# Halved additions on GpSimd, and the next tile's x turned between context and out-projection

## The reference

```
xn  = layernorm(x)
# attention branch, on xn
q, k, v = split(rmsnorm(xn) * norm1_w @ qkv_w + qkv_b)      # 16 heads of 16
q, k    = relu(q), relu(k), each times cos and sin of the position
ctx     = causal linear attention:  q . cumsum(k v) / (q . cumsum(k) + eps)
h       = xn + ctx @ out_w + out_b
m       = h + gelu((rmsnorm(h) * norm2_w) @ mlp_w1 + mlp_b1) @ mlp_w2 + mlp_b2
# ternary branch, on xn
f       = relu(xn @ Wfc.T + gate * low_rank(xn)) ** 2 @ Wproj.T
out     = x + m + f
```

## Time and profile before

| what | value |
|---|---|
| time, median of 3 runs | 640.94 us (640.76 to 641.73) |
| the profiled execution: time, span | 644.8 us, 641.9 us |
| TensorE busy | 589.1 us (92% of the span), granted clock 0.988 |
| VectorE / ScalarE / GpSimd busy | 421.8 / 367.5 / 217.9 us (66, 57, 34%) |
| HBM traffic | 26 GB/s over the span |

### The profile page before, as it was taken

One profiled execution on the slowest core, in us unless ns is written; L12 is line 12 of the kernel. 1 busy time (PEld: TensorE's weight loads), 2 busy tenths in 40 slices (PEclk: granted clock), 3 DMA queues, 4 the chain that ended last, 5 costly groups with the idle time before them and its releaser, 6 DMA issues.

```text
span 641.9 us, 14501 instructions
## 1 busy us (share of the span) xinstructions
PE 589.1 (92%) x5070; PEld 515.2 (80%) x5070; DVE 421.8 (66%) x776; ACT 367.5 (57%) x654; POOL 217.9 (34%) x219
## 2 busy tenths in 40 slices
PE   2757999989999999999999999999999999999986
PEld 2646878978888888888889887888879888888876
DVE  7689966477655766477664876558674786647542
ACT  5465583546745566465845657455754658455643
POOL 6006333153233432153432432334420533333220
PEclk9969999989999999999999999999999999999999
DMA  7771005600065002620056000740036200540000
GB/s 205 213 188 49 17 1 128 137 2 19 1 150 113 16 0 66 121 74 16 0 122 113 26 16 14 148 100 16 0 90 106 65 16 0 135 94 2 2 1 33
DMA packets 27992, 42.01 MB, mean 65 GB/s; under 512 B 9008, under 2 KB 19904, under 8 KB 27968
## 3 DMA queue, kind: packets, MB, share of 16 engines
q1 hardware_dynamic: 26528, 39.59, 26.7%
q10 hardware_dynamic: 1440, 2.10, 1.2%
HBM read 12.31 MB, written 4.19 MB: 26 GB/s over the span
## 4 chain that ended last, share of the span: by engine, by line
PE 78%; DVE 8%; ACT 6%; issue 2%; SPq 2%; ACTq 1%; DMA 1%; POOL 0%; DVEq 0%
PE accum L1194 20%; PE dense L1179 8%; PE dense L1356 8%; PE shared L1217 5%; DVE wide_lo L945 5%; PE ctx_ps L1242 5%; PE dense L1229 4%; PE dense L1090 4%; PE dense L1361 4%; PE shared L1330 4%; PE shared L1104 3%; PE ctx_ps L1253 2%; PE dense L1094 2%; PE dense L1184 2%; PE upd_ps L1267 2%
## 5 line engine op out<-in xcount | busy, mean ns | idle before, releaser
L945 DVE TENSOR_TENSOR wide_lo<-wide,wide_hi 128x512 fp32r<-128x512 f32 x128 | 116.7, 913 | 81.3 <-ACT wide_hi L672 74.4
L484 POOL TENSOR_TENSOR arena<-arena,tab 128x256 f32<-128x256 f32 x64 | 50.1, 804 | 142.3 <-DMA q_stack<-arena 142.3
L953 DVE TENSOR_TENSOR weighted<-shared,cst 128x512 f32<-128x512 f32 x128 | 82.8, 683 | 18.1 <-PE shared L1217 17.9
L669 ACT ACTIVATE wide<-dense,b 128x512 f32<-128x512 f32 x64 | 44.1, 690 | 80.6 <-PE dense L1361 80.2
L510 POOL TENSOR_TENSOR state<-state,added 128x544 f32<-128x544 f32 x32 | 43.6, 1363 | 115.5 <-DVE added L975 115.5
L1194 PE MATMUL accum<-w_hi,wide_hi 128*128 128x256 f32 x256 | 73.5, 287 | 8.0 <-DVE wide_lo L945 8.0
L1194 PE MATMUL accum<-prT,wide_hi 128*128 128x256 f32 x256 | 66.7, 287 | 6.8 <-DVE wide_lo L945 6.8
L1194 PE MATMUL accum<-w_lo,wide_hi 128*128 128x256 f32 x256 | 71.9, 281 | 0.0
L1194 PE MATMUL accum<-w_hi,wide_lo 128*128 128x256 f32 x256 | 71.8, 280 | 0.0
L659 ACT ACTIVATE wide<-dense,scales 128x512 f32<-128x512 f32 x64 | 44.1, 689 | 43.4 <-PE dense L1184 35.4
L1194 PE MATMUL accum<-prT,wide_lo 128*128 128x256 f32 x256 | 65.2, 281 | 0.0
(11 more groups left out here) (166 smaller groups left out, 1438.5 us busy)
## 6 DMA issues: line engine op xcount, KB each, us to landing
k_stack<-weighted SPq DMA_DIRECT2D x96, 128.0 KB, 2.7
q_stack<-arena SPq DMA_DIRECT2D x184, 64.0 KB, 2.3
xin<-L_attn_x SPq DMA_DIRECT2D x16, 256.0 KB, 2.9
out<-late SPq DMA_DIRECT2D x16, 256.0 KB, 2.3
tab<-trig SPq DMA_DIRECT2D x8, 258.0 KB, 2.7
arena<-L_ffn_w_fc SPq DMA_DIRECT2D x1, 1024.0 KB, 8.5
late<-L_ffn_w_proj SPq DMA_DIRECT2D x1, 1024.0 KB, 7.0
late<-L_attn_mlp_w ACTq DMA_DIRECT2D x1, 1024.0 KB, 5.5
```

The source lines that it names most:

```text
L484: pool.tensor_tensor(q_trig[:, j % 2, r, :, :], qT[:, :, k * P:(k + 1) * P], row.broadcast_to([P, KE, P]), ALU.mult).then_inc(q_trig_done, 1)
L669: act.activation(wide[:, m % 2, :], dense[m % 2][:, :], ACT.Gelu_apprx_tanh, bias=b1[:, m:m + 1]).then_inc(dense_free, 1)
L945: dve.tensor_tensor(wide_lo[:, n % 2, :], wide[:, n % 2, :], wide_hi[:, n % 2, :].bitcast(F32), ALU.subtract).then_inc(lo_done, 1)
L953: dve.tensor_tensor(weighted[:, g, :].rearrange("p (a n) -> p a n", a=4), shared[g % 2][:, :].rearrange("p (a n) -> p a n", a=4), mask.rea ...
```

## The change

What it does, part by part. (1) The four additions of 128 x 1024 on GpSimd are made in halves of 128 x 512, and each half waits until VectorE has done a named `split`: `xn + ob` is made in chunks 1 and 2 instead of ahead of chunk 0; the other six halves stand behind the splits of the MLP blocks 1 to 6. The ternary result goes into `res` and no longer waits for `xb + ctxn`. (2) Turning x of the next tile moves from behind `mlp_up(0)` to between `ffn_up(7)` and the out-projection, and writes the context and update banks (`ctx_ps`, `upd_ps`) instead of `shared`. (3) The four k and q blocks of the next tile move from around `mlp_down(0)`: the first ahead of the turning of h, the second behind it, the two of q behind `ffn_down(7)`; `make_z` moves to behind `mlp_up(1)`. `ffn_down(4)` is no longer halved, and `ffn_up(6)` and `ffn_up(7)` move ahead of and behind the turning of the context. (4) The statistics of the next x move to the very start of the tile on VectorE, the moments behind chunk 0 and the inverse root to chunk 1, `scale_x` on ScalarE into chunk 3 (tile 0: one chunk later, statistics and moments together). (5) SyncE loads x two tiles ahead of its use, behind the 36 stacking DMAs of a tile instead of at its start. Squares and hs are written into `xn` instead of `xs`.

The diff, cut to its core:

```
@@ constants
-        N_SHARED = 26
+        N_SHARED = 24
-        MLP_BEFORE_KQ = 2
...
+        def x_bank(t, m):
+            return shared[m] if isinstance(t, int) and t == 0 else (ctx_ps, upd_ps)[m]
@@ SyncE
+            load_next_x(0)
-            def body(t, more):
+            def body(t, more, more_x):
                 if more:
-                    sp.wait_ge(xn_done, (t + 1) * NB)
-                    sp.wait_ge(xb_done, t + 1)
-                    sp.wait_ge(xs_done, (t + 1) * NB)
-                    load_x(t + 1)
                     sp.wait_ge(q_trig_done, (t + 1) * 2 * NB)
                     sp.wait_ge(v_trig_done, (t + 1) * 2 * NB)
                     load_tab(t + 1)
                     stack(t + 1)
+                if more_x:
+                    load_next_x(t + 1)
@@ GpSimd
-                pool.tensor_tensor(xn[:, :, :], xn[:, :, :],
...
+                def xn_plus_ob(j):
+                    pool.wait_ge(xn_done, (t + 1) * NB)
+                    pool.wait_ge(lo_done, t * 2 * HB + j + 2)
+                    two = slice(2 * j - 2, 2 * j)
...
+                    if 1 <= j <= 2:
+                        xn_plus_ob(j)
+                    if more and j == (2 if isinstance(t, int) and t == 0 else 1):
+                        inverse_root(t + 1)
...
-                if more:
-                    inverse_root(t + 1)
...
+                def behind_split(m):
+                    pool.wait_ge(lo_done, t * 2 * HB + HB + m + 1)
-                pool.tensor_tensor(res, xb[:, :, :], ctxn, ALU.add).then_inc(res_done, 1)
...
-                pool.tensor_tensor(res, res, ctxn, ALU.add).then_inc(res_done, 1)
+                for g in range(2):
+                    behind_split(1 + g)
+                    pool.tensor_tensor(xb[:, two, :], xb[:, two, :], ctxn[:, two, :], ALU.add).then_inc(res_done, 1)
+                for g in range(2):
+                    behind_split(3 + g)
+                    pool.wait_ge(ffn_done, t * NB + 2 * g + 2)
+                    pool.tensor_tensor(res[:, two, :], res[:, two, :], xb[:, two, :], ALU.add).then_inc(res_done, 1)
                 if more:
                     keep_msq(t + 1)
-                    x_plus_b2(t + 1)
+                    for g in range(2):
+                        behind_split(5 + g)
+                        x_plus_b2(t + 1, g)
@@ ScalarE
                 for j in range(NB):
                     if j + 1 < NB:
                         trig_v(j + 1)
+                    elif more:
+                        scale_x(t + 1)
                     read_context(j)
                     ffn_block(j + 2)
...
                 ffn_block(6)
+                if more:
+                    x_hi(t + 1)
...
                 ffn_block(7)
+                if more:
+                    relu_block(t + 1, 0)
...
                 if more:
-                    scale_x(t + 1)
+                    for i in range(1, 2 * KE):
+                        relu_block(t + 1, i)
@@ VectorE
                 if not isinstance(t, int) or t:
+                    if more:
+                        ln_statistics(t + 1, range(NB))
                     v_rows(t, 1)
...
-                    if more:
-                        ln_statistics(t + 1, ((), (0,), (1,), (2, 3))[j])
+                    if isinstance(t, int) and t == 0:
+                        if j == 1:
+                            ln_statistics(t + 1, range(NB))
+                            moments(t + 1)
+                    elif j == 0 and more:
+                        moments(t + 1)
                 context(NB - 1)
-                if more:
-                    moments(t + 1)
+                split(5)
...
+                    if more:
+                        x_lo_half(t + 1, g)
...
+                if more:
+                    k_parts_split(t + 1)
                 dve.wait_ge(wide_used, t * 2 * HB + HB)
-                dve.wait_ge(res_done, t * 2 + 1)
...
                 if more:
-                    x_lo(t + 1)
+                    q_parts_split(t + 1)
@@ TensorE
-                ffn_down(4, (0, 1))
+                ffn_down(4)
+                ffn_up(6)
...
-                ffn_up(6)
-                ffn_down(4, (2, 3))
+                ffn_up(7)
+                if more:
+                    turn_x(t + 1)
...
                 ffn_down(5)
-                ffn_up(7)
                 ffn_down(6)
+                if more:
+                    make_kq(t + 1, 0, (0,))
...
-                mlp_up(0, (0,))
+                if more:
+                    make_kq(t + 1, 0, (1,))
                 ffn_down(7)
-                mlp_up(0, (1,))
                 if more:
-                    turn_x(t + 1)
+                    make_kq(t + 1, 1)
+                mlp_up(0)
                 for m in range(1, HB):
                     mlp_up(m)
-                    if m == MLP_BEFORE_KQ - 1 and more:
-                        make_kq(t + 1, 0)
+                    if m == 1 and more:
+                        make_z(t + 1)
                     mlp_down(m - 1)
```

More of the change, by code:

```diff
@@ L312, in mlp_place @@
         def mlp_place(m, more):
-            return HB + m + (2 * KE if m >= MLP_BEFORE_KQ and more else 0)
+            return HB + m + (2 * KE if more else 0)
         def mlp_use(t, m, more):
@@ L428, in body @@
                                  res[:, 2 * b:2 * b + 2, :]).then_inc(out_sent, 16)
-            body(0, True)
-            with sp.Fori(1, NT - 1) as t:
-                body(t, True)
-            body(NT - 1, False)
+            body(0, True, True)
+            with sp.Fori(1, NT - 2) as t:
+                body(t, True, True)
+            body(NT - 2, True, False)
+            body(NT - 1, False, False)
             sp.wait_ge(out_sent, NT * 32)
@@ L533, in body @@
                     pool.wait_ge(x_in, t * 32 + 64)
-                    x_plus_b2(t + 1)
+                    for g in range(2):
+                        behind_split(5 + g)
+                        pool.wait_ge(res_done, t * 4 + 3 + g)
+                        x_plus_b2(t + 1, g)
             body(0, True)
@@ L594, in relu_block @@
                                bias=qkb[:, base + m:base + m + 1]).then_inc(dense_free, 1)
-            def relu_kq(t):
-                if not isinstance(t, int) or t:
-                    act.wait_ge(q_trig_done, t * 2 * NB)
-                for i in range(2 * KE):
-                    relu_block(t, i)
             scale_x(0)
@@ L719, in body @@
                 if more:
-                    scale_x(t + 1)
+                    for i in range(1, 2 * KE):
+                        relu_block(t + 1, i)
                 for m in range(HB):
                     mlp_block(m)
-                    if m == 0 and more:
-                        x_hi(t + 1)
-                    if m == MLP_BEFORE_KQ - 1 and more:
-                        relu_kq(t + 1)
-                if more:
-                    z_hi(t + 1)
+                    if m == 1 and more:
+                        z_hi(t + 1)
             body(0, True)
@@ L963, in context @@
                     if j == 0:
-                        later(dve, res_done, t * 2)
+                        later(dve, res_done, t * 4)
                     dve.tensor_tensor(ctxn[:, chunk_block(j), :].rearrange("p (h e) -> p h e", e=D), heads[:, :, 0:D],
@@ L1011, in body @@
                                       ALU.subtract).then_inc(shared_free, 1)
-                split(5)
-                dve.wait_ge(xnb_done, t + 1)
+                split(6)
+                dve.wait_ge(xnb_done, 2 * (t + 1))
                 for g in range(2):
@@ L1018, in body @@
                                       xn[:, 2 * g:2 * g + 2, :].rearrange("p b n -> p (b n)"), ALU.add).then_inc(shared_free, 1)
[L1019 removed]
+                    if more:
+                        x_lo_half(t + 1, g)
                 for k in range(NB):
                     dve.wait_ge(r2_done, t * 4 + k // 2 * 2 + 2)
[L1022 removed]
+                    dve.tensor_scalar(xn[:, k, :], ctxn[:, k, :], r2[:, k:k + 1], None, ALU.mult).then_inc(hs_done, 1)
                 split(7)
@@ L1067, in turn_x @@
                 for m in range(KE):
-                    use = shared_use(t, m - KE)
-                    if not isinstance(t, int) or t:
-                        pe.wait_ge(shared_free, use - 1)
+                    if m and (not isinstance(t, int) or t):
+                        pe.wait_ge(upd_free, t * N_UPD)
                     for k in range(NB):
-                        mm = pe.transpose(shared[m][:, k * P:(k + 1) * P], xs[:, k, m * P:(m + 1) * P], ident)
-                    mm.then_inc(shared_full, 1)
+                        mm = pe.transpose(x_bank(t, m)[:, k * P:(k + 1) * P], xs[:, k, m * P:(m + 1) * P], ident)
+                    mm.then_inc(x_turned, 1)
             def dense_bank(use, n):
@@ L1078, in dense_bank, with make_kq @@
                 return dense[n % 2]
-            def make_kq(t, which):
-                for i in range(KE * which, KE * which + KE):
```

(4 more changed lines are left out.)

80 lines of the change are left out of this document (41 added, 39 removed).

## The result

The changed kernel takes 623.84 us (median of 4 runs, 623.03 to 624.36), the kernel before 641.34 beside it (640.76 to 643.51): 0.9716 of it, 95% interval 0.9697 to 0.9735. That is 17.5 us less by the medians; forecast were 21.7 less (619, range 611 to 630). The profiled execution took 624.36 us with a span of 622.6; its span is 19.3 shorter than that of before.

A forecast was written before the change was run, and what follows sets the result against it. TensorE bounds the kernel: back-to-back matmuls plus four pauses a tile. Gains of 5 x 2.5 in inner tiles, 2.5 + 3.0 in tile 1 and 3.7 in tile 0 sum to 21.7: 640.9 becomes 619 us, range 611 to 630.

The forecast's parts named there:

- A: TensorE's pause ahead of the first ternary down product, 0.61 us a tile; to become about 0.15, gain 0.46.
- D: TensorE's pause ahead of the down product of MLP block 2, 1.01 us a tile; to go wholly, gain 1.01.
- B: TensorE's pause ahead of the turning of the context, 0.50 us a tile; to be covered by moved blocks, gain 0.50.
- C: TensorE's pause ahead of the first MLP product, 0.99 us a tile; to be covered by moved blocks, gain 0.99.
- Term (a): Nine moments, 1.24 us, ahead of chunk 0's division on VectorE: new pause of 0.27 at `across` of chunk 1.
- Term (b): VectorE's chain to the first MLP split ends 13.6 us after the out-projection: new pause of 0.5 ahead of `mlp_down(0)`.
- Rival B: VectorE's chain to the first MLP split becomes the bound, costing 2 us instead of 0.5; 629 us, chance 0.18.
- x: Load of the next x behind the 36 stackings, landing about at the tile's end: no cost, about 1 us slack.
- Rival D: x lands late, 6.2 us into the tile; first down product pauses 4.4 us a tile; 645 us, chance 0.04.
- Tile 1: Gains 2.5 like inner tiles plus 3.0, as its longer pause ahead of the first ternary down product and clock drop go.
- Tile 0: Net gain 3.7 us: 3.0 from shorter splits, less 1.8 for statistics and moments holding `across` of chunk 2, plus 2.5.
- Rival C: The waits of B and C reappear at `scale_x` or the banks; only the halves' 13.0 us remains; 628, chance 0.10.

The follow-up runs named there:

- experiment 1: Also `m_before_update`: the changed kernel with the nine moments ahead of the masking of the update of chunk 0 in the loop's tiles; 616.67 us, 0.9612 of before.
- experiment 2: Also `trig_earlier`: the changed kernel with GpSimd making chunk 2's `trig_q` ahead of the addition into chunk 0's state, in the loop's tiles; 618.80 us, 0.9645 of before.
- experiment 9: The changed kernel with SyncE loading the next x behind the two stores of the output instead of ahead of them; 660.39 us, 1.0291 of before.
- experiment 7: The kernel before run once more with no edit; 641.22 us over 8 runs.
- whole_additions: The changed kernel with part (1) undone, the four GpSimd additions whole and at their old places; 635.34 us, 0.9890 of before.
- halves_only: The kernel before with part (1) alone, the four GpSimd additions in halves; 625.92 us, 0.9740 of before.

## Why the prediction was right, and where it was not

**The mechanism** was right: TensorE's pauses were what could be had, halving and moving the additions frees the splits (A, D), and the moved blocks cover B and C. The time lies in the range, and in the forecast's own 615 to 624, at its upper end. That the sum of an inner tile is nearly right (2.33 for 2.5) is in part luck: two of its terms were off in opposite ways.

**Term (a), the moments**: mis-sized, 0.27 forecast, 1.1 measured (experiment 1). The step that failed is their price of 1.24, taken from a place where GpSimd was quiet; beside `trig_q` they take 2.1 (experiment 2). The prediction named this hold for the splits and did not ask it of the moments.

**Term (b), VectorE's chain**: 0.5 forecast, about 0.1 measured. TensorE's cover was right: 13.06 from the end of the out-projection at about 374.05 makes 387.11, and the matmul stands at 387.19. The chain ends 0.9 earlier than forecast: the last part of q ends at 386.05, 12.0 behind the out-projection, which with a split is 12.7, not 13.6. What then ends last is ScalarE's rounding of MLP block 0. Rival B, which rested on this chain, did not come: its own condition, an item over 1 us late, was not met, and even 0.73 more cost 0.2.

**Pause A**: 0.15 was to stay, nothing did.

**x**: "cost nothing, with a slack of about 1 us" holds in tiles 3 to 6 and fails in tiles 1 and 2 (0.87 each). The price of 22.7 us for the stackings came from a tile of the steady state; in the first two they took 1.4 to 1.9 more, most of it in one or two single issues. Why is open; the kernel before shows it too (8.01 and 15.43 us ahead of its tile 1), so "each issue took 0.63 all along" was not so. In tile 2 this made x late; in tile 1 it was a landing of 4.4 us, for which the prediction took 2.9, the median.

**Rival D** did not come, but experiment 9 shows that its price was right. Counted as the prediction counts, from the first ternary up product, x let VectorE begin 6.23 us into the tile in experiment 9, the 6.2 that it assumed, and TensorE stood for 4.42, where it forecast 4.4. In tile 1 of the changed kernel it was 2.69 us (121.78 less 119.09, where the first up product stands) and 0.88, so that the loss begins at 1.8, and the 2.5 gained are used up at 4.3 ("about 4"). What waits is the third scores, not the first down product, which comes out the same. Its 645 lacked the clock: behind pauses of 4.1 to 4.7 us the drop cost 1.4 to 2.1 a tile more.

**Tile 1**: 5.5 forecast, 4.4 in the profile. The 1.1 that are missing are x (0.88) and the 0.17 that every inner tile gained less. Of the 4.4, some 1.6 are the drop of the clock, which some executions of before do not have: tile 1 is 1.86 shorter in experiment 7, of which the shorter pause is 0.30. The prediction saw no drop behind any other pause inside a tile, "all of them shorter"; that is misread, since tile 0's pause of 2.44 is longer and no drop followed it. "A saved pause is as long in both" fails with the drop: the profiled spans differ by 19.3, the medians by 17.5. How often the drop comes was not counted.

**Tile 0** (3.7, measured 3.8): its parts came out near the working. With the halves alone it takes 75.74 instead of 79.26, so they are worth 3.5 there (3.0); `whole_additions` (78.8 instead of 75.5) can't be read for this, since the clock fell in its tile 0. The statistics and moments hold `across` of chunk 2 by 1.39 of idle (1.8).

**Rival C** had what the halves bring alone right but for 2: 625.9 against 628. The 2 are the 1.8 that it took off for the statistics in tile 0, which `halves_only` does not pay. It is not what happened: B and C went, and most of their gain was given back to the moments, to x and in tile 0.

## What to carry to other kernels

Price a small VectorE instruction at the place to which it goes, beside what GpSimd does there; two additions of 128 x 4 cost 0.86 us here, nearly as much as pause D (1.01), which the halves were made to remove. When a change with several parts brings less than its parts, look for the pauses it made, not for those it left: here one line moved gave 7 us back. A load that heads an engine's list of a tile needs slack against the slowest issue and the slowest landing seen, not against the medians. And before two counts of time are compared, see that they start at the same instruction.

## What the runs showed of the hardware

A hold by GpSimd ends with the single instruction, not with the run of them, and it also catches tiny operands: 0.15 us became 0.70. Pauses of TensorE of 4.1 to 4.7 us cost 1.4 to 2.1 us more by the clock in each tile; of two pauses of 2.43 and 2.44 us at the same place one was followed by the drop (granted clock 0.61 in the next 2 us) and one was not (1.00). Of the twelve stackings of k one took 1.76 us to issue ahead of tile 1 and one 1.69 ahead of tile 2, and of the 24 of q one 1.34, where the median is 0.60 and 0.59 and none is longer than that by more than 0.01 later on; what held these three the trace does not show. One load of x took 4.4 us to land ahead of tile 1, where the others took 2.7 to 3.2; this too came in some executions only (4.1 in `m_before_update`, 2.9 in `trig_earlier`).
